# A four-layer network in ten programs in place of seventeen: the start, the joints before self attention, and the experts

## The chip, the cores and the metric

One core of one Trainium2 chip runs the kernel. The metric is the device time of one execution in microseconds (us). The engines are TensorE (PE: matmuls; PEld: its weight loads), VectorE (DVE), ScalarE (ACT), GpSimd (POOL) and SyncE (SP), which here issues all DMAs. Each engine has its own stream of instructions; they meet at semaphores only. A *program* below is one block of five such streams, closed by a barrier over all engines.

## The reference, cut to what matters

The input is x of 8 batches x 256 tokens x 128 features, a condition vector per batch and a context of 8 x 1601 x 128. Layer 0 is, in short:

```python
c_proj = silu(c) @ W_mod + b_mod            # six vectors per batch: shift, scale, gate
x = x + gate_a * (self_attention(modulate(_ln(x), shift_a, scale_a)) @ W_proj + b_proj)
q_c  = _ln(x) @ W_qc + b_qc                 # 16 heads of 8
kv_c = _ln(context) @ W_kvc + b_kvc         # 1601 keys; only this layer normalises the context
x = x + cross_attention(q_c, kv_c) @ W_cproj + b_cproj
x = x + gate_m * (gelu(modulate(_ln(x), shift_m, scale_m) @ W_mlp1 + b_mlp1) @ W_mlp2 + b_mlp2)
```

Layer 1 has rotary positions in the self attention; layer 2 has shifted windows of 64 tokens there (masks), the 16 largest scores alone in the cross attention, and a gated MLP. Layer 3 is

```python
nx = layer_norm(x)
evidence = softmax((nx @ Wq) @ (context @ Wk).T * H**-0.5) @ (context @ Wv)    # one head
combined = concat([nx, evidence, anchor])
router_probs = softmax(combined @ router_W + router_b)                          # three experts
h = silu(combined @ e_w1 + e_b1);  expert_out = h @ e_w2 + e_b2
routed = sum(expert_out * router_probs)
g = sigmoid(silu(combined @ gate_w1 + gate_b1) @ gate_w2 + gate_b2)
out = x + g * (routed @ out_w + out_b)
```

## The kernel before, in words

x stays in SBUF, features on the 128 partitions and 2048 tokens along the columns, worked on in NC = 4 chunks of CH = 512 columns (two batches each). `program` (L2474) runs the stages one after the other, each a program of its own: for each layer `stage_load` (L183: weights, vectors, the modulation vectors), in layer 0 `stage_context_norm` (L248), `stage_project` (L504: the norm of x, the projections to q, k and v, the split of q and k into three bf16 parts), `stage_attention` (L958) for the self attention and again for the cross attention, and `stage_mlp` (L1430: output projection of the cross attention, norm, MLP). Layer 2's cross attention, its MLP and layer 3 up to the evidence are one program, `stage_last` (L1626); then come `stage_load` for layer 3 and `stage_experts` (L2329). q and k go through DRAM (`q_dram`, `k_dram`), and before also v (`v_dram`), since the attention wants them in another layout.

The context norm works batch by batch with two buffers (`cn_raw`, b % 2), 13 tiles of 128 keys. SP loads batch b as soon as the norm and the transposition of b-2 are done, then stores batch b-1 behind its evictions. DVE takes the statistics of b (L292, L296, L299, L301), waits for ScalarE's square root (L324), and normalises b in place:

```python
nc.vector.reciprocal(rv[:, k, :], rv[:, k, :]).then_inc(ve_r.sem, 1)
dve.wait_ge(rstd_r.sem, rstd_r.at(b + 1))
for j in range(NT):
    last = nc.vector.tensor_scalar(raw[:, k, j, :], raw[:, k, j, :], mv[:, k, j, 0:1], rstd[:, k, j:j + 1],
                                   ALU.subtract, ALU.mult)
last.then_inc(norm_r.sem, 1)
```

PE then transposes the 13 tiles (L317), ScalarE evicts them (L331), SP stores them to `ctxn_dram` (L271). The rows of constants that the attention stages need are written by memsets: two on DVE of 10.73 us each (L225) and two on POOL of 13.89 us together (L203) in `stage_load` of layer 0.

In `stage_last` the order of the work is written out by hand: `LastOrder` gives each item of the layer-3 chain of batch b a step (b starts at step 52 b + 72; the evidence loop of scores `x3`, values and denominators is one item per step), and every engine runs through the steps in the same order, its score work first, then the items. Score work of the cross attention ends with step 415 of 416 steps; the chains of batches 6 and 7 run on alone behind it. `stage_experts` takes the four chunks in order; each is 15 uses of a ring of seven PSUM banks: router r0 to r2, then per expert two hidden blocks h (Silu) and an output y, then the gate g1 (Silu), g2 (Sigmoid) and the output o, 28 matmuls of 128x512 in all. The router's exponential (L2419) comes behind r2.

Of the kernel before, what the change touches and what calls it, by code (L numbers as in the profile page):

```python
# [104 lines left out]
class Program:  # L105
    def __init__(self, nc, ctx, io):
# [12 lines left out]
        self.vec = self.sb("vec", [P, V_MAX])  # L119
        self.modv = self.sb("modv", [P, 9, B])  # L120
# [5 lines left out]
        self.v_dram = dram("v_dram", (B, P, 2, NH * VW), F32)  # L126
# [44 lines left out]
def vector(p, layer, name, n=0):  # L171
    at = V_OFF[layer][0][name] + n
    return p.vec[:, at:at + 1]


def stage_load(p, layer):

    nc, (w_off, n_w), (v_off, n_v) = p.nc, W_OFF[layer], V_OFF[layer]
    loaded, act_ready, mm_ready, mod_ready, rows_set = (p.sig(s) for s in ("w_loaded", "cact_ready", "mod_mm", "mod_ready", "rows_set"))
    n_mod = dict(L_WEIGHTS[layer]).get("mod", 0)  # L180
    n_dma = 2 + (5 if layer == 0 else 0)
    scale_slots = [] if layer == 3 else [m[layer][0] for m in (MOD_SELF, MOD_CROSS, MOD_MLP) if m[layer][0] is not None]
    with ExitStack() as ctx:  # L183
        mod_ps = p.ps(f"mod_ps{layer}", [P, 9, B], ctx)
        block = ctx.enter_context(nc.Block())

        @block.sync
        def _(sp):
            sp.dma_start(p.w[:, 0:n_w, :], p.io[f"w{layer}"]).then_inc(loaded.sem, 16)
            sp.dma_start(p.vec[:, 0:n_v], p.io[f"v{layer}"]).then_inc(loaded.sem, 16)  # L190
            if layer == 0:
                sp.dma_start(p.cond[:], p.io["cond"]).then_inc(loaded.sem, 16)
                sp.dma_start(p.const[:], p.io["const"]).then_inc(loaded.sem, 16)
                sp.dma_start(p.neg_id[:], p.io["neg_id"]).then_inc(loaded.sem, 16)
                sp.dma_start(p.id_bf[:], p.io["id_bf"]).then_inc(loaded.sem, 16)
                sp.dma_start(p.x[:], p.io["x"]).then_inc(loaded.sem, 16)
            sp.wait_ge(loaded.sem, loaded.at(16 * n_dma))

        if layer == 0:
            @block.gpsimd  # L200
            def _(pool):
                for hf in range(2):
                    nc.gpsimd.memset(p.q_st[64 * hf + 32:64 * hf + 64], 0.0).then_inc(rows_set.sem, 1)  # L203
                pool.wait_ge(rows_set.sem, rows_set.at(2))
# [2372 lines left out]
```

## Time and profile before

| | |
|---|---|
| time, median of 3 runs | 4627.36 us (4610.62 to 10193.9) |
| the profiled execution | 4624.74 us, span 4623.0 us |
| load and context norm | 0 to 113.3 |
| projection 0, first score of self 0 | 113.3 to 160.1, 166.84 |
| cross 0 ends; MLP 0, load 1, projection 1, first score of self 1 | 956.6; to 1012.4, 1024.3, 1088.7, 1095.5 |
| cross 1 ends; MLP 1, load 2, projection 2, first score of self 2 | 1940.8; to 1998, 2011, 2057.5, 2073.8 |
| the last program: score work, batch 6's and 7's chains | to 4323, 4459.4 |
| load 3 and anchors; four expert chunks | to 4473.6; 4623.0 |
| busy | PE 3625.3, DVE 3536.7, ACT 2945.9, POOL 691.4 us |

Times are positions in the profiled execution, from the start of its span. A profile row gives start and duration of an instruction (a run of equal ones in one row with x and their number), its engine and line, what it writes and reads, and in brackets the idle time of the engine before it and what ended it. SPq is SP's issue of a DMA, not the transfer. A 32-bit matmul shows as two records. The granted clock is a share of TensorE's full 2.4 GHz. The profiled execution is near the median.

### The profile page before, as it was taken

To read this page: it belongs to the slowest core of one execution; us is meant where nothing else is said; L and a number is where in the kernel's file an instruction comes from. 1 tells how busy PE (TensorE), PEld (TensorE's weight loads), DVE (VectorE), ACT (ScalarE), POOL (GpSimd) and SP (SyncE) were. 2 spreads that over 40 slices of the span, in tenths; PEclk is the share of its full clock that TensorE was granted. 3 is DMA by queue.
4 is the path that set the end of the run, shared out by engine and by line. 5 is a ranking of instruction groups with operands and counts; after the bars stand their busy time and mean duration, and the time that the engine had idled before them with its cause. 6 is when DMAs were issued, how large, how long until landed. Compare 5 with 4: busy or idle time off the path is not lost. (4 is left out here: it accounts for less than half of the span.)

```text
span 4623.0 us, 75349 instructions
## 1 busy us (share of the span) xinstructions
PE 3625.3 (78%) x28388; PEld 1609.1 (35%) x28388; DVE 3536.7 (77%) x5424; ACT 2945.9 (64%) x5480; POOL 691.4 (15%) x1464
## 2 busy tenths in 40 slices
PE   2769999976789999858367778787787878778877
PEld 2323333332323333323132334334343434334543
DVE  7658989826568888537699998898989889898213
ACT  1556888844647878627377776767677677766413
POOL 1322122004234242013011010000101000000000
PEclk7788999987879999878666677777777667766769
DMA  4553353205434333144311011110111011000000
GB/s 138 147 132 85 85 112 84 57 22 144 120 91 95 90 94 80 24 107 118 80 36 43 22 29 37 31 34 19 40 30 37 18 32 34 13 12 10 13 19 9
DMA packets 277795, 280.05 MB, mean 61 GB/s; under 512 B 38960, under 2 KB 252472, under 8 KB 276536
## 3 DMA queue, kind: packets, MB, share of 16 engines
q1 hardware_dynamic: 277432, 275.22, 23.9%
q8 instruction: 226, 3.70, 0.4%
q14 instruction: 137, 1.12, 0.1%
HBM read 149.53 MB, written 124.43 MB: 59 GB/s over the span
## 5 line engine op out<-in xcount | busy, mean ns | idle before, releaser
L1369 DVE TENSOR_REDUCE mpart<-ring 128x1 f32<-128x400 f32 (+2 forms) x2816 | 1293.0, 524 | 273.9 <-PE ring L1156 267.1
L1287 ACT ACTIVATE prob<-xa_ps 128x512 f32<-128x512 f32 (+1 forms) x2048 | 1109.8, 596 | 243.5 <-PE xa_ps L1201 223.1
L2068 ACT ACTIVATE prob<-x_ps 128x512 f32<-128x512 f32 (+1 forms) x832 | 451.9, 598 | 313.3 <-PE x_ps L1926 246.5
L1156 PE MATMUL ring<-k_st,q_st 52*128 52x400 bf16 (+2 forms) x2560 | 580.7, 340 | 43.2 <-DMA k_st<-k_dram 11.3
L1790 PE MATMUL ring<-k_st,q_st 52*128 52x400 bf16 (+1 forms) x1024 | 330.5, 444 | 294.2 <-ACT s_sb L2004 276.3
L1220 PE MATMUL xa_ps<-prob,va 128*9 128x256 f32 x6656 | 506.4, 383 | 0.4 <-ACT prob L1287 0.4
L2283 DVE MAX8 mpart<-s_sb 128x8 f32<-128x1601 f32 x256 | 456.1, 1817 | 61.5 <-ACT s_sb L2004 61.5
L2004 ACT ACTIVATE s_sb<-ring 128x400 f32<-128x400 f32 (+1 forms) x1024 | 468.2, 517 | 40.1 <-PE ring L1790 31.8
L1995 ACT ACTIVATE un<-s_sb 128x1601 fp8e4<-128x1601 f32 x256 | 392.9, 1536 | 128.8 <-DVE s_sb L2292 128.3
L2286 DVE MATCH_REPLACE8 s_sb<-mpart,s_sb 128x1601 f32<-128x1601 f32 x256 | 461.9, 1812 | 0.0
L2292 DVE MATCH_REPLACE8 s_sb<-m8b,s_sb 128x1601 f32<-128x1601 f32 x256 | 461.8, 1812 | 0.0
L2289 DVE MAX8 m8b<-s_sb 128x8 f32<-128x1601 f32 x256 | 454.6, 1816 | 0.0
L1201 PE MATMUL xa_ps<-q_st,k_st 55*128 55x256 bf16 (+1 forms) x3840 | 408.6, 279 | 56.7 <-ACT prob L1287 43.5
L1921 PE MATMUL x_ps<-neg_id,un 128*128 128x128 bf16 (+1 forms) x3328 | 349.9, 268 | 47.0 <-ACT prob L2068 46.1
L1921 PEld LDWEIGHTS x_ps<-neg_id,un 128*128 128x128 fp8e4 (+1 forms) x3328 | 286.3, 128 | 188.6 <-ACT prob L2068 131.0
L1943 PE MATMUL av_ps<-prob,va 128*9 128x256 f32 (+1 forms) x3328 | 338.2, 496 | 0.0
L1156 PEld LDWEIGHTS ring<-k_st,q_st 52*128 52x128 bf16 x2560 | 180.1, 95 | 408.5 <-DVE mpart L1369 259.6
L1790 PEld LDWEIGHTS ring<-k_st,q_st 52*128 52x128 bf16 x1024 | 84.8, 112 | 511.8 <-ACT s_sb L2004 387.3
L1201 PEld LDWEIGHTS xa_ps<-q_st,k_st 55*128 55x128 bf16 (+1 forms) x3840 | 142.3, 96 | 314.1 <-ACT prob L1287 287.4
L1926 PE MATMUL x_ps<-q_st,k_st 55*128 55x256 bf16 (+1 forms) x1664 | 210.1, 342 | 0.0
L1271 ACT ACTIVATE mT<-ring 24x128 bf16<-24x128 bf16 x160 | 41.9, 262 | 211.9 <-PE ring L1162 210.3
L1220 PEld LDWEIGHTS xa_ps<-prob,va 128*9 128x9 f32 x6656 | 105.3, 88 | 188.8 <-issue 108.2
(291 smaller groups left out, 4195.3 us busy)
## 6 DMA issues: line engine op xcount, KB each, us to landing
k_st<-kc_dram SPq DMA_DIRECT2D x192, 300.2 KB, 5.5
o_dram<-o_sb SPq DMA_DIRECT2D x192, 128.0 KB, 1.8
kc_dram<-k SPq DMA_DIRECT2D x72, 300.0 KB, 3.4
ctx_t<-in_ctxT SPq DMA_DIRECT2D x24, 800.5 KB, 4.8
q_st<-q_dram SPq DMA_DIRECT2D x80, 192.0 KB, 4.2
kc_dram<-k SPq DMA_DIRECT2D x72, 200.0 KB, 3.9
k_st<-k_dram SPq DMA_DIRECT2D x48, 192.0 KB, 5.0
kc_dram<-k SPq DMA_DIRECT2D x24, 300.8 KB, 3.3
```

Of the source, the lines that this page charges most:

```text
L1156: nc.tensor.matmul(ring_ps[:, r % BANKS, 0:w], q_st[rows, b % NQ, 2 * t + pl, qt * P:(qt + 1) * P], k_st[rows, slot_of(n), pl, c0:c0 + w], ...
L1201: last = nc.tensor.matmul(x_ps[0:sizes[j], (2 * s + hf) % XBANKS, pl * T:(pl + 1) * T], k_st[rows, slot_of(n), pl, keys], q_st[rows, b % N ...
L1220: last = nc.tensor.matmul(av_ps[32 * k:32 * k + VW, n % 2, :], va[0:sizes[j], b % NVB, j, G * t + k, :], prob[0:sizes[j], s % NPROB, (2 * ...
L1287: nc.scalar.activation(prob[0:size, s % NPROB, hf * 512:(hf + 1) * 512], x_ps[0:size, (2 * s + hf) % XBANKS, :], ACT.Exp, scale=HEAD_SCALE ...
L1369: nc.vector.tensor_reduce(mpart[:, n % 4, row, c:c + 1], ring_ps[:, r % BANKS, 0:chunks[c][1]], AX.X, ALU.max).then_inc(g["red"].sem, 1)
L1921: nc.tensor.matmul(x_ps[0:sizes[j], (2 * s + hf) % XBANKS, pq * P:(pq + 1) * P], un[:, n % 2, hf * G + pq, keys], p.neg_id[:], start=pq == ...
L2004: nc.scalar.activation(s_sb[:, q % 4, c0:c0 + w], ring_ps[:, r % BANKS, 0:w], ACT.Copy).then_inc(g["rout"].sem, 1)
L2068: nc.scalar.activation(prob[0:size, s % NPROB, hf * 512:(hf + 1) * 512], x_ps[0:size, (2 * s + hf) % XBANKS, :], ACT.Exp, scale=HEAD_SCALE ...
L2283: ins = nc.vector.max(best, sc)
L2286: ins = nc.vector.match_replace(sc, best, sc, -BIG)
L2289: ins = nc.vector.max(m8b[:, half, :], sc)
L2292: ins = nc.vector.match_replace(sc, m8b[:, half, :], sc, -BIG)
```

## The change

Three parts.

**The start.** `stage_begin` replaces `stage_load` of layer 0 and `stage_context_norm`. SP loads context batches first and puts constants, weights and x between them; POOL does all memsets; the modulation matmuls follow batch 6. The norm goes to ScalarE as Identity with scale = 1/std and bias = -mean/std; DVE computes that bias (`shifts`) in two small operations:

```diff
-                for j in range(NT):
-                    last = nc.vector.tensor_scalar(raw[:, k, j, :], raw[:, k, j, :], mv[:, k, j, 0:1], rstd[:, k, j:j + 1],
-                                                   ALU.subtract, ALU.mult)
-                last.then_inc(norm_r.sem, 1)
+            def shifts(b):
+                k = b % 2
+                dve.wait_ge(rstd_r.sem, rstd_r.at(b + 1))
+                if b >= 2:
+                    dve.wait_ge(norm_r.sem, norm_r.at(b - 1))
+                nc.vector.tensor_scalar(mv[:, k, :, 0], mv[:, k, :, 0], -1.0, None, ALU.mult).then_inc(shift_r.sem, 1)
+                dve.wait_ge(shift_r.sem, shift_r.at(2 * b + 1))
+                nc.vector.tensor_tensor(shift[:, k, :], mv[:, k, :, 0], rstd[:, k, :], ALU.mult).then_inc(shift_r.sem, 1)
+
+            for b in range(B + 1):
+                if b < B:
+                    statistics(b)
+                if b >= 1:
+                    shifts(b - 1)
...
         @block.scalar
+            for b in range(B):
+                k = b % 2
+                act.wait_ge(ve_r.sem, ve_r.at(2 * b + 2))
+                nc.scalar.activation(rstd[:, k, :], rv[:, k, :], ACT.Sqrt).then_inc(rstd_r.sem, 1)
+                if b >= 1:
+                    evict(b - 1)
+                act.wait_ge(shift_r.sem, shift_r.at(2 * b + 2))
+                for j in range(NT):
+                    last = nc.scalar.activation(raw[:, k, j, :], raw[:, k, j, :], ACT.Identity, bias=shift[:, k, j:j + 1], scale=rstd[:, k, j:j + 1])
+                last.then_inc(norm_r.sem, 1)
```

SP's order per batch b is unchanged in kind: load b (behind norm and transposition of b-2), then the store of b-1, which waits for its evictions. DVE's instructions from the start of the context norm, before:

```order
L292 BN_STATS cn_st<-cn_raw 128x6 [waits cn_in1]
L292 BN_STATS cn_st<-cn_raw 128x6 x12
L296 BN_AGGR cn_mv<-cn_st 128x2 [waits cn_stats]
L296 BN_AGGR cn_mv<-cn_st 128x2 x12
L299 TENSOR_SCALAR cn_rv<-cn_mv 128x13 [waits cn_aggr]
L301 RECIPROCAL cn_rv<-cn_rv 128x13 [waits cn_ve]
L304 TENSOR_SCALAR cn_raw<-cn_raw,cn_mv,cn_rs 128x128 [waits cn_rstd]
L304 TENSOR_SCALAR cn_raw<-cn_raw,cn_mv,cn_rs 128x128 x12
```

and of the change, from the statistics of batch 1 on (`cn_in1` is the load of an odd batch, `cn_in0` of an even one):

```order
L248 BN_STATS cn_st<-cn_raw 128x6 [waits cn_in1]
L248 BN_STATS cn_st<-cn_raw 128x6 x12
L252 BN_AGGR cn_mv<-cn_st 128x2 [waits cn_stats]
L252 BN_AGGR cn_mv<-cn_st 128x2 x12
L255 TENSOR_SCALAR cn_rv<-cn_mv 128x13 [waits cn_aggr]
L257 RECIPROCAL cn_rv<-cn_rv 128x13 [waits cn_ve]
L265 TENSOR_SCALAR cn_mv<-cn_mv 128x13 [waits cn_rstd]
L267 TENSOR_TENSOR cn_sh<-cn_mv,cn_rs 128x13 [waits cn_shift]
L248 BN_STATS cn_st<-cn_raw 128x6 [waits cn_in0]
```

The 13 normalising operations are gone from DVE, and the two operations L265 and L267 that stand behind the statistics of batch 1 belong to batch 0.

**Between cross and self stages.** One class `Between` and `stage_between` (L691 of the change) replace `stage_mlp`, `stage_load` and `stage_project`. Its levels run over the four chunks one after the other:

```diff
+    HEAD = ("op", "mean", "var", "diag", "norm", "mod", "up", "down")
+    TAIL = ("mean", "var", "diag", "norm", "proj")
...
+            if self.layer is not None:
+                sp.wait_ge(s["mm"].sem, s["mm"].at(self.at["down", NC - 1] + 1))
+                sp.dma_start(p.w[:, free:n_w, :], p.io[f"w{nxt}"][:, free:n_w, :]).then_inc(s["w2"].sem, 16)
```

All ups come before all downs, through four PSUM banks (before two for the ups and one for the downs, an up and a down of neighbouring chunks in turn). The next layer's weights up to the cross output block are loaded at its start, those that the MLP itself still uses at its end (they serve later stages); vectors and modulation have two places each (`layer % 2`). v stays in SBUF (`vs`), the masks of layer 2 and the first two batches' q and k are loaded in it. On SP, in the joint before self 0, the change has

```order
L156 DMA q_dram<-bt_parts 128x512
L674 DMA q_st<-q_dram 48x8x256 [waits on_st0]
L674 DMA q_st<-q_dram 48x8x256
L683 DMA k_st<-k_dram 48x8x256 x2
L674 DMA q_st<-q_dram 48x8x256 x2
L683 DMA k_st<-k_dram 48x8x256 x2
L156 DMA q_dram<-bt_parts 128x3x512 [waits pj_parts]
```

where before these loads opened the next program. The first line ends the q store of chunk 2, the last begins that of chunk 3; three more stores of k follow.

**The experts beside the last batch.** `LastOrder` gets the expert uses as items of its steps, and `stage_last` the streams of `stage_experts`:

```diff
+        self.experts, self.stores = {}, {}
+        self.weights = self.STEPS * B + 1
+        for c in range(NC):
+            at = self.STEPS * B + 10 + c * N_EXPERT if c < NC - 1 else self.end
+            for n in range(N_EXPERT):
+                self.put(self.experts, at + n, (c, n))
+            self.put(self.stores, at + N_EXPERT + 1, c)
+        self.end += N_EXPERT + 2
```

STEPS x B is 416 and N_EXPERT 15: chunks 0 to 2 take steps 426 to 470, one use a step; batch 6's evidence loop has steps 423 to 437, batch 7's chain 436 to 470 and its loop 474 to 489; chunk 3 comes behind the last evidence. The weights go to the place of the keys (`k_flat`) behind the last score. The expert's intermediate tiles lie in buffers that the scores no longer use, with four PSUM banks (`xa_ps`) in place of seven. The exponential of the router follows h of expert 0 instead of r2. PE in batch 7's chain, before (L1837 and L1844 are its links: root, norm, MLP, mean, variance):

```order
L1837 MATMUL ring<-ls_hid,w 128x256 x4
L1837 MATMUL ring<-x,const 128x256
L1844 MATMUL ring<-const,ls_sqd 128x1 x2
L1837 MATMUL ring<-ls_sqd,const 128x256
```

and in the change (L1838 and L1845 are the same links, L1994 is an expert use, its weights in `k_st` or `s_sb`):

```order
L1838 MATMUL ring<-ls_hid,w 128x256 x4
L1994 MATMUL xa_ps<-nx_190,k_st 128x512
L1994 MATMUL xa_ps<-o_all,k_st 128x512
L1994 MATMUL xa_ps<-prob,k_st 128x512
L1994 MATMUL xa_ps<-s_sb,k_st 128x512
L1838 MATMUL ring<-x,const 128x256
...
L1845 MATMUL ring<-const,ls_sqd 128x1 x2
```

Between two links there are now two to six expert matmuls. On ScalarE, in batch 6's loop, the change reads (L2082 is the loop's exponential, L2159 an expert's Silu or a router logit)

```order
L2082 ACTIVATE ls_hid<-ring 128x256
L2159 ACT_TABLE_LOAD
L2159 ACTIVATE un<-xa_ps,prob 128x256 x2
L2165 ACT_TABLE_LOAD
L2165 ACTIVATE s_sb<-s_sb 128x1536
L2082 ACTIVATE ls_hid<-ring 128x256
L2159 ACT_TABLE_LOAD
L2159 ACTIVATE un<-xa_ps,prob 128x256 x2
L2082 ACT_TABLE_LOAD
L2082 ACTIVATE ls_hid<-ring 128x256 x2
```

where before the loop's exponentials followed one another. From there to the end ScalarE has 26 table loads, before 14.

## Rows read from the trace of the kernel before

**Rows 1.** Page, part 2: the granted clock in 40 slices, tenths of full speed.
```profile
PEclk7788999987879999878666677777777667766769
```

**Rows 2.** Six stretches: start:end length, busy us (x instructions) per engine, clock, DMA share, GB/s.
```profile
28.40:113.30 84.90, 24.23 (x104) 21.09 (x104) 58.98 (x328) 18.67 (x41) 3.51 (x3) 0.70 0.52 155
1012.80:1024.30 11.50, 2.70 (x12) 2.64 (x12) 0.52 (x4) 0.21 (x1) 0.00 (x0) 0.59 0.42 149
4323.00:4333.00 10.00, 7.37 (x41) 2.65 (x39) 4.76 (x9) 1.13 (x3) 0.98 (x5) 0.99 0.09 27
4333.00:4371.00 38.00, 37.94 (x106) 24.50 (x106) 0.35 (x1) 4.61 (x13) 0.72 (x1) 0.50 0.08 26
4414.00:4459.40 45.40, 42.91 (x121) 28.10 (x121) 0.59 (x2) 7.01 (x16) 0.61 (x1) 0.51 0.00 0
4546.00:4581.00 35.00, 26.48 (x57) 11.00 (x58) 13.97 (x15) 14.60 (x27) 0.00 (x0) 0.95 0.02 8
```

**Rows 3.** Timeline of the context norm, batches 1 to 3: start, us, engine, line, operation.
```profile
45.65 0.38 SPq L267 DMA_DIRECT2D cn_raw<-in_ctx  x1
...
52.34 2.61 DVE L292 BATCH_NORM_STATS2 cn_st<-cn_raw 128x6 f32<-128x128 f32 x13 [3.14 <-DMA cn_raw<-in_ctx]
...
56.20 0.24 DVE L301 RECIPROCAL cn_rv<-cn_rv 128x13 f32<-128x13 f32 x1
56.73 3.42 DVE L304 TENSOR_SCALAR cn_raw<-cn_raw,cn_mv,cn_rs 128x128 f32<-128x128 f32 x13 [0.28 <-ACT cn_rs L324]
...
63.85 0.34 SPq L271 DMA_DIRECT2D ctxn_dram<-cn_o  x1
...
64.29 0.38 SPq L267 DMA_DIRECT2D cn_raw<-in_ctx  x1
```

**Rows 4.** Groups of instructions by form, ScalarE, context norm and projection: busy us, mean ns.
```profile
L331 ACT ACTIVATE cn_o<-cn_ps 128x128 f32<-128x128 f32 x8 | 2.2, 272 | 0.0
...
L414 ACT ACTIVATE n_h<-n_xc,modv 128x256 f32<-128x256 f32 x8 | 4.3, 590 | 3.5 <-DVE n_xc L395 3.5
```

**Rows 5.** Timeline at the joints before self 0, self 1 and self 2, single instructions.
```profile
128.72 1.45 PE L556 MATMUL pj_ps<-n_h,w 128*128 128x512 f32 x3
...
156.03 1.57 SPq L164 DMA_DIRECT2D k_dram<-pj_q  x3
...
160.11 0.86 SPq L1036 DMA_DIRECT2D q_st<-q_dram  x2
...
166.84 0.61 PE L1156 MATMUL ring<-k_st,q_st 52*128 52x256 bf16 x4 [5.68 <-DMA k_st<-k_dram]
...
978.12 1.45 PE L1463 MATMUL ml_ps<-n_h,w 128*128 128x512 f32 x3
...
1011.66 0.69 DVE L1496 TENSOR_TENSOR x<-x,ml_res 128x512 f32<-128x512 f32 x1
...
1024.44 1.19 PE L361 MATMUL n_mean<-x,const 128*128 128x512 f32 x1 [0.92 <-PEq L183]
...
1039.93 1.45 PE L556 MATMUL pj_ps<-n_h,w 128*128 128x512 f32 x3
...
1080.43 0.69 DVE L608 TENSOR_TENSOR pj_q<-pj_f,pj_q 128x512 bf16<-128x512 f32 x1
...
1084.56 1.69 SPq L164 DMA_DIRECT2D k_dram<-pj_q  x3
...
2026.48 1.02 PE L556 MATMUL pj_ps<-n_h,w 128*128 128x512 f32 x2
...
2057.59 1.32 SPq L1029 DMA_DIRECT2D q_masked<-in_qmask  x4
...
2073.79 0.61 PE L1156 MATMUL ring<-k_st,q_masked 52*128 52x256 bf16 x4 [15.15 <-DMA k_st<-k_dram]
```

**Rows 6.** Timeline of ScalarE in the tail: a table load and what follows it.
```profile
4386.47 1.28 ACT L2013 ACT_TABLE_LOAD   x1
4387.76 0.47 ACT L2013 ACTIVATE ls_hid<-ring,vec 128x256 f32<-128x256 f32 x1
```

More of the change, by code:

```diff
@@ L539, in _ @@
[L539 to L543 removed]
+            bt.sp(sp)
         @block.tensor
         def _(pe):
[L547 to L556 removed]
@@ L557, in _ @@
-            for g in range(NV):
-                m = NI * stepn + g
-                if g < 3:
-                    pe.wait_ge(pf.sem, pf.at(m - 2))
-                else:
-                    pe.wait_ge(v_out.sem, v_out.at(g - 2))
-                for k in range(4):
-                    last = nc.tensor.matmul(pp[:, m % 3, k * P:(k + 1) * P], norm.h[:, g, k * P:(k + 1) * P], weight(p, layer, "v"), start=True, stop=True)
-                last.then_inc(v_mm.sem, 1)
+            bt.pe(pe)
         @block.scalar
@@ L627, in stage_project @@
-    pf.passed(NI * stepn)
-    for name, mine in turn.items():
-        chain[name].passed(len(mine) * (PER - 1))
-        parts[name].passed(len(mine))
-    stored.passed(16 * len(RUNS) * NI)
-    norm.done()
+            bt.pool(pool)
+    bt.done()
 class Onward:
@@ L900, in by_step, with stage_attention @@
     return out
-def stage_attention(p, layer, kind):
+def stage_attention(p, layer, kind, vs=None, q_self=None):
     nc = p.nc
     cross = kind == "cross"
-    masked = layer == 2 and not cross
     rope = layer == 1
@@ L1519 @@
+N_EXP = 3
+EXPERT_USES = [("r", e, "act") for e in range(N_EXP)]
+for expert in range(N_EXP):
+    EXPERT_USES += [("h", (expert, 0), "act"), ("h", (expert, 1), "act"), ("y", expert, "dve")]
+EXPERT_USES += [("g1", 0, "act"), ("g2", 0, "act"), ("o", 0, "dve")]
+N_EXPERT = len(EXPERT_USES)
 class LastOrder:
@@ L1946, in values, with anchors @@
                 last.then_inc(g["av"].sem, 1)
+            def anchors():
+                pe.wait_ge(g["exp"].sem, g["exp"].at(2 * END))
+                pe.wait_ge(g["ocopy"].sem, g["ocopy"].at(NU))
+                pe.wait_ge(x["w"].sem, x["w"].at(32))
+                pe.wait_ge(x["rw"].sem, x["rw"].at(1))
+                for k in range(10):
+                    if k < 3:
+                        w = e_rw[:, 6 + k, :]
+                    elif k < 9:
+                        w = w_e("ew1", (k - 3) // 2 * 6 + 4 + (k - 3) % 2)
+                    else:
+                        w = w_e("gw1", 2)
+                    last = nc.tensor.matmul(xa_ps[:, 0, k * B:(k + 1) * B], w, p.cond[:], start=True, stop=True)
+                last.then_inc(x["mm"].sem, 1)
@@ L1962, in _ @@
                     values3(b, j)
+                for c, n in order.experts.get(k, []):
+                    if (c, n) == (0, 0):
+                        anchors()
+                    expert(c, n)
         @block.scalar
@@ L2260, in between @@
                     evidence(b)
+                if k == order.weights:
+                    expert_begin()
+                for c, n in order.experts.get(k, []):
+                    if (c, n) == (0, 0):
+                        expert_anchors()
+                    expert_in(c, n)
             def slot(k):
```

1171 lines of the change are left out of this document (561 added, 610 removed).

## The prediction

> **What bounds the kernel now.** I read the page's first two parts, then the chain that ended last, then a table by stretches, and last single instructions in order of time. TensorE's granted clock moves between full and near half over the span [rows 1]. The change leaves the inner loops of the attention stages alone (some 4,000 of the 4,623 us) and rebuilds four places: the start, the three joints before a self attention, and the tail. So I read what ends last in each. In the context norm it is a round trip of load, statistics, norm and transposition, with every engine idle in part: DVE 59 us, PE 24, ACT 19 of 85 us [rows 2]. At the joints a small stage waits for DMAs: the weight load of layer 1 takes 11.5 us for 2.70 us of PE [rows 2]. In the tail first one batch's loop, then the other's, runs on PE at half clock, and the four expert chunks follow alone, the third of them in 35 us [rows 2].
>
> **The start.** Before, a load of batch b is issued (45.65), its statistics start 6.69 us later (52.34), the reciprocal ends at 56.44, the norm on DVE runs from 56.73 to 60.15, and the next store and load are issued at 63.85 and 64.29 [rows 3]. Two batches are in flight, so that this chain of 18.6 us gives two batches, 9.4 us each. What changes is where the norm waits. ScalarE needs the shift of batch b-1, and DVE computes it behind the statistics of b; these wait for load b; SP issues load b+1 only behind the store of b-1, which waits for that norm and its transposition. Nothing of two batches overlaps any more, and each batch pays for the whole chain:
> load to statistics 6.9 (mean of three, 6.69 one of them), statistics to reciprocal 4.10, the two shift operations with their wait 0.5, the norm on ScalarE, and norm end to next load 4.14 [rows 3].
> The norm on ScalarE is 13 operations of 128x128 with scale and bias from columns. No such operation is in the trace. Below it lies the plain copy of 128x128, 0.272; above it the 128x256 with scale and bias, 0.590 alone, which holds twice the columns [rows 4]. In a row of several the latter takes 0.51. I take 0.40, nearer the second because of its two columns; 5.2 us for 13, ends 3.5 and 6.6. It replaces 3.42 on DVE. By the Trainium skill, page "ScalarE: Activation LUTs", a fixed cost and 0.83 ns per column with some 93 ns per pointer operand would make it about 5.0 us, an estimate; this case's rows only enclose it.
> Period: 6.9 + 4.1 + 0.5 + 5.2 + 4.1 = 20.8 us. Load 2 can go out at 24.2 (first statistics at 6.1, second to 14.3, norm 0 to 20.0, 4.1 more). Load 7 goes out five periods later, plus 7 us that the weights (1.4 MB) and x (1 MB) cost on the queue ahead of loads 4 and 6: 135.2. Its statistics, shift, sqrt, the eviction of batch 6, ScalarE's norm with its table switches, and the last store with 3.9 of landing end the program at 168.6. Before, the same point is 113.3 [rows 2], the 28.4 us of the load stage included. **+55.3.** The memsets, now all on POOL, cost nothing: it does nothing else in these 168 us, and together they are some 55 (as long as the two engines took for them before); without that cover a part of these 55 would stand ahead of the first projection.
> Bounds: with the norm at 3.5 or 6.6 the eight periods give -12 or +10.
>
> **The joint before self 0.** The projection starts at 128.72, the last k store is issued at 156.03, the next stage opens at 160.11 and its first score runs at 166.84 [rows 5]: 27.3 + 4.1 + 6.7 = 38.1 us. After, v stays in SBUF, so that no v store stands before the last k store on SP (but eight q and k loads of the first two batches do, 3.7 us, so that I put it at 25.4); those loads land inside the program, and the first score needs only 1.7 after the barrier: 25.4 + 4.2 + 1.7 = 31.3, **-6.8**. The start and this joint together: first score at 215.3 in place of 166.84, +48.5.
>
> **The joint before self 1.** The weights of the next layer load under the MLP. The gap between x ready (1012.35) and the next mean (1024.44) [rows 5] goes: -12.1, of which 2.70 of modulation returns ahead of the up matmuls [rows 2]. All 16 ups before all 16 downs, through four banks in place of two, take 27.3 (32 matmuls of 0.853, if no wait is left) instead of the 34.2 us from 978.12 to 1012.35 [rows 5]: -7.0, and with the modulation the MLP ends 4.4 earlier. The norm that follows need not start at half clock (0.59 in the load stage [rows 2]): I put 13 in place of 15.5, -2.5. From the projection on: from 1039.93 to the k store at 1084.56 44.6, + 4.2 + 6.7 = 55.5 [rows 5]. Now the store goes as soon as DVE has split (1081.12, 41.2), + 4.2 + 1.7 = 47.1: -8.4. Sum -12.1 - 4.4 - 2.5 - 8.4 = **-27.5**.
>
> **The joint before self 2.** The same gap; the MLP with the modulation gains only 1.9, for its first ups are slow for the clock, and that stays. The gap of 13.3 us goes, mean to projection takes 13 in place of 15.4, and x is ready 1.9 earlier: the projection starts at 2008.9 in place of 2026.48, -17.6. Then the masks, four large broadcasts that SP issues first from 2057.59 and that hold the first score till 2073.79 (16.2 us instead of 6.7) [rows 5], move under the MLP: 31.3 in place of 47.3, -16.0. **-33.6.** Cover gone, the masks would cost 9.5.
>
> **The tail.** Before: batch 6's loop ends near 4371, batch 7's chain near 4459.4 [rows 2], load and anchors to 4473.6, four chunks to 4620.5, output to 4623.0. After, chunks 0 to 2 lie between the steps of batches 6 and 7, and the barrier, weight load (9 us) and anchor wait are gone. In three pieces from 4333:
> A, batch 6's loop with anchors and 24 of chunk 0's 28 matmuls. The loop's 37.94 us of PE at clock 0.50 [rows 2] become 19 at full clock, 2.5 more until it rises; anchors 4.4; 24 x 0.853 = 20.5 (a chunk is 28 matmuls, 23.9 of 26.5 busy in its window [rows 2]); waits for softmax and tables some 10. 56 us: 4389.
> B, batch 7's chain to its top scores: 16.7 of PE at full clock, 60 expert matmuls 51.2, waits 13. 81: 4471. The chain's own waits, some 12 us before, lie under expert matmuls.
> C, batch 7's loop, alone and at half clock as before, 47.4 [rows 2]: 4518.5.
> Chunk 3 alone as the last chunk before, 37.8, and the output 2.5: 4558.5.
> Against 4623.0, **-64.5**, ends -35 (30 us of waits more) and -80 (C at a higher clock).
>
> **Sum:** 4623.0 + 48.5 - 27.5 - 33.6 - 64.5 = 4545.9 of span; the profiled execution is 1.74 above its span, so 4547.6, say **4548**, 1.7% under. Against the median 4627.36 the profiled 4624.74 is 0.06% lower, which I neglect.
>
> **Rivals.**
> *ScalarE's table switches hold PE.* In the tail the instruction order has 26 table loads where it had 14, and 16 lie in A and B. A load takes 1.28 us and the next operation starts 0.01 us after it [rows 6], so I count 1.28. If PE waits 2 us more at each of the 16, the tail is 32 longer: 4565 to 4580. For it: in a chunk PE already waits some 7 us for the hidden layer's activations. Against: ScalarE is busy only 14.6 of 35 us [rows 2]. Chance 0.17. The Trainium skill, same page, section "What ACT_TABLE_LOAD costs", adds a drain of about 1,380 ns to the 1,283 of the load; by it the 16 switches make about 22 us, 4570. The rows here show the load's figure and no gap behind it, and the measurement decides.
> *TensorE stays at 1.2 GHz in A and B.* The loop at 4333 ran at 0.50 although the stretch ahead of it was at 0.99, and batch 7's at 0.51, while the third expert chunk got 0.95 [rows 2]. If the mixture is granted what the loop alone was, A becomes 24 longer and B 68: 4640, **slower than before** by 15. It decides once the lower level costs more than 79 us of these 92. Against: more than half of PE's work in A and B is of the kind that ran at 0.95. Chance 0.06 for both, 0.12 for A alone (4572).
> *The start is not serial.* If load b overlaps the norm of b-1, the start costs 15 less than before and not 55 more: about 4480. The order shows the shift behind the statistics, so only 0.04.
> *Fewer waits in the tail, or the clock higher in C:* 4520 to 4535, chance 0.22.
> My forecast with its terms' own scatter, 4535 to 4565, 0.39.
>
> **The numbers.** The likeliest case gives 4548. The range takes in the better tail and the table switches and A alone: 4505 to 4598; outside lie the 1.2 GHz case, the overlapping start and some ends of the terms. Two per cent, about what a measurement of this kernel can tell from no change, is 92.5 us: 4534.8 and 4720. Faster by more: the overlapping start, most of the better tail, and an edge of the forecast, where the start's norm is cheaper: 0.36. Slower by more takes the 1.2 GHz case and a term lost besides: 0.02. The rest, 0.62.
>
> **What would show it.** Right: statistics in the new start begin about 21 us apart, with ScalarE's 13 operations near 5.2; first scores at about 215, and at the joints 27 and 34 us earlier than the shift of the start leaves them; chunk matmuls among batch 7's at a clock near 0.9, and a last chunk of 37 to 38. Wrong: statistics less than 15 apart (the start pipelines), a long idle of PE behind table loads in A and B, or a granted clock near 0.5 from 4333 to the last chunk. A change in the inner loops of the attention stages, of which I expect none, would undo the sum altogether: v now read from one SBUF tensor and ten in place of seventeen programs could move them, and a tenth of a per cent of them is 4 us.

## The result, and the profile after

The changed kernel takes 4593.23 us (median of 19 runs, 4575.58 to 4611.64) against 4630.73 us of the kernel before (19 runs, 4602.85 to 4647.76 but for one of 10193.9, which the ratio leaves out): ratio 0.9925, 95% interval 0.9907 to 0.9942. It is 0.75% faster, clear of noise, where 1.7% was forecast. The profiled execution has a span of 4603.4 us, against the 4545.9 of the sum. It lies in the upper part of its runs, so that the two spans differ by less (19.6 us) than the medians (37.5). The stretches that the change rebuilds repeat better than the total: in the profiles of all kernels below that leave them alone, the first score of self 0 comes at 242.3 to 245.3, the joints take 116.0 to 118.8 and 100.5 to 102.0, the tail 236.1 to 236.2. The attention stretches do not: that of self attention 0 alone lies between 168.6 and 180.2. The comparison goes by stretch:

| stretch | before | predicted | after | after - predicted |
|---|---|---|---|---|
| start to the first score of self 0 | 166.8 | 215.3 | 244.8 | +29.5 |
| self and cross attention 0 | 790.2 | same | 787.8 | -2.3 |
| joint before self 1 (end of cross 0 to first score) | 138.5 | 111.0 | 116.9 | +5.9 |
| self and cross attention 1 | 845.7 | same | 847.2 | +1.6 |
| joint before self 2 | 132.7 | 99.1 | 101.4 | +2.3 |
| layer 2 to batch 6's evidence loop | 2259.3 | same | 2269.2 | +9.9 |
| tail, from that loop on | 289.9 | 225.4 | 236.2 | +10.8 |

The largest miss, half of all, is in the start. DVE's row there, in order of time (the first two batches; columns as in [rows 3], which they answer):

```profile
9.15 0.97 DVE L252 BATCH_NORM_AGGREGATE cn_mv<-cn_st 128x2 f32<-128x6 f32 x13
10.15 8.74 DVE L255 TENSOR_SCALAR cn_rv<-cn_mv 128x13 f32<-128x13 f32 x1
18.93 0.24 DVE L257 RECIPROCAL cn_rv<-cn_rv 128x13 f32<-128x13 f32 x1
19.08 2.55 DVE L248 BATCH_NORM_STATS2 cn_st<-cn_raw 128x6 f32<-128x128 f32 x13
...
22.67 3.20 DVE L255 TENSOR_SCALAR cn_rv<-cn_mv 128x13 f32<-128x13 f32 x1
25.90 0.24 DVE L257 RECIPROCAL cn_rv<-cn_rv 128x13 f32<-128x13 f32 x1
26.06 10.63 DVE L265 TENSOR_SCALAR cn_mv<-cn_mv 128x13 f32<-128x13 f32 x1
36.73 0.17 DVE L267 TENSOR_TENSOR cn_sh<-cn_mv,cn_rs 128x13 f32<-128x13 f32 x1
53.24 2.61 DVE L248 BATCH_NORM_STATS2 cn_st<-cn_raw 128x6 f32<-128x128 f32 x13 [16.34 <-DMA cn_raw<-in_ctx]
```

and POOL's, over the same time:

```profile
1.12 6.92 POOL L235 MEMSET q_st<- 32x8192 bf16 x1
8.10 10.76 POOL L237 MEMSET k_st<- 32x12808 bf16 x1
18.92 6.92 POOL L235 MEMSET q_st<- 32x8192 bf16 x1
25.89 10.77 POOL L237 MEMSET k_st<- 32x12808 bf16 x1
```

Three operations of 128x13 that need 0.1 to 0.2 us last 8.74, 3.20 and 10.63 us, and each ends within 0.04 us of the end of a memset: 10.15 + 8.74 = 18.89 beside 8.10 + 10.76 = 18.86, 22.67 + 3.20 = 25.87 beside 25.84, 26.06 + 10.63 = 36.69 beside 36.66. The statistics between them (19.08, over while a memset runs) are untouched, and so is the reciprocal (18.93, 0.24 us), though it has one tensor input too. What waits is TENSOR_SCALAR, one tensor and a constant. The third batch's statistics start at 53.24; the working has them at 31.1 (load at 24.2, 6.9 more). From there on the start does what was worked out. ScalarE's 13 operations take

```profile
36.94 5.11 ACT L325 ACTIVATE cn_raw<-cn_raw,cn_sh,cn_rs 128x128 f32<-128x128 f32 x13 [17.52 <-DVE cn_sh L267]
```

and the statistics:

```profile
73.97 2.61 DVE L248 BATCH_NORM_STATS2 cn_st<-cn_raw 128x6 f32<-128x128 f32 x13 [16.39 <-DMA cn_raw<-in_ctx]
...
118.79 2.61 DVE L248 BATCH_NORM_STATS2 cn_st<-cn_raw 128x6 f32<-128x128 f32 x13 [16.40 <-DMA cn_raw<-in_ctx]
```

53.24 to 73.97 is 20.7 us (predicted 20.8), 5.11 us for the norm (predicted 5.2, between bounds of 3.5 and 6.6). No weights and no x are loaded ahead of these two batches.

The joints, lines that answer to [rows 5]: the projection of self 0, and the first scores of self 0, 1 and 2.

```profile
206.96 1.88 PE L477 MATMUL bt_bank<-bt_h,w 128*128 128x512 f32 x4
...
244.80 0.61 PE L1214 MATMUL ring<-k_st,q_st 52*128 52x256 bf16 x4
...
1149.52 0.61 PE L1214 MATMUL ring<-k_st,q_st 52*128 52x256 bf16 x4
...
2098.10 0.61 PE L1214 MATMUL ring<-k_st,q_masked 52*128 52x256 bf16 x4
```

From projection to first score 37.8 us where 31.3 was put. From SP's first store to the barrier the DMA view of this stretch (40 slices of 0.74 us, busy tenths and GB/s) reads

```profile
DMA  0699999999999999999999999999999999999940
GB/s 0 208 346 327 350 343 346 322 344 340 335 343 346 328 344 348 315 218 241 177 145 176 176 146 179 155 167 177 146 183 291 386 380 382 382 385 389 382 159 0
```

Between the first and the last slices the DMA engines are never idle: some 340 GB/s in the first stores, about 170 (145 to 241) while the loads pass, and some 380 in seven of the last slices, where the last stores land.

The tail, by stretches (columns as in [rows 2]): batch 6's loop with the anchors and, at its end, the first two expert matmuls; the loop with expert matmuls between its items; batch 7's chain with chunks; its loop alone; chunk 3.

```profile
4367.20:4384.40 17.20, 17.15 (x49) 11.22 (x50) 0.50 (x2) 1.53 (x4) 0.00 (x0) 0.50 0.07 20
4384.40:4418.50 34.10, 32.29 (x118) 18.44 (x117) 9.39 (x8) 22.06 (x33) 0.72 (x1) 0.96 0.05 19
4418.50:4518.40 99.90, 83.58 (x239) 42.17 (x237) 41.69 (x59) 48.04 (x85) 5.78 (x10) 0.95 0.02 8
4518.40:4559.00 40.60, 40.17 (x117) 27.11 (x117) 0.17 (x1) 6.26 (x15) 0.08 (x1) 0.52 0.00 0
4559.00:4603.40 44.40, 31.05 (x58) 12.47 (x58) 14.07 (x15) 16.06 (x27) 0.53 (x1) 0.85 0.02 6
```

Once expert matmuls lie between, the same loop is granted 0.96 where it had 0.50 [rows 2]. The chain with chunks is too long, and its waits are PE's for ScalarE (us in all, times, longest):

```profile
PE xa_ps L1994 <- ACT un L2159: 10.6, 4, 4.3
```

### The profile page after: what moved, and what is told of

The parts are those of the page before. It is cut to its first block, busy times and chain, and to the rows that moved or that the text cites. A ratio compares the mean times of both kernels' runs of the same rounds, so it can differ in the third digit from the quotient of the medians.

```text
span 4603.4 us, 75234 instructions
## 1 busy us (share of the span) xinstructions
PE 3604.8 (78%) x28389; PEld 1598.2 (35%) x28389; DVE 3511.9 (76%) x5334; ACT 2997.1 (65%) x5593; POOL 714.8 (16%) x1466
## 4 chain that ended last, share of the span: by engine, by line
DVE 20%; PE 17%; ACT 10%; issue 3%; POOL 0%; ACTq 0%; POOLq 0%; DVEq 0%
DVE m8b L2448 6%; DVE s_sb L2445 5%; ACT un L2048 5%; DVE s_sb L2451 4%; DVE mpart L2442 3%; PE xa_ps L1922 2%; PE xa_ps L1994 2%; PE ring L1838 2%; ACT prob L2121 2%; PE xa_ps L1944 2%; PE xa_ps L1927 2%; PE ring L1868 2%; ACT s_sb L2057 1%; PE e_ps L1880 1%; PE ring L1791 1%
## 5 line engine op out<-in xcount | busy, mean ns | idle before, releaser
L1343 ACT ACTIVATE prob<-xa_ps 128x512 f32<-128x512 f32 (+1 forms) x2048 | 1109.9, 596 | 245.2 <-PE xa_ps L1259 224.1
L2121 ACT ACTIVATE prob<-xa_ps 128x512 f32<-128x512 f32 (+1 forms) x832 | 452.0, 598 | 313.6 <-PE xa_ps L1927 246.4
L1259 PE MATMUL xa_ps<-q_st,k_st 55*128 55x256 bf16 (+1 forms) x3840 | 408.5, 279 | 54.7 <-ACT prob L1343 43.7
L1922 PE MATMUL xa_ps<-neg_id,un 128*128 128x128 bf16 (+1 forms) x3328 | 351.3, 269 | 46.7 <-ACT prob L2121 45.8
L1922 PEld LDWEIGHTS xa_ps<-neg_id,un 128*128 128x128 fp8e4 (+1 forms) x3328 | 287.1, 128 | 190.8 <-ACT prob L2121 133.4
L1944 PE MATMUL xa_ps<-prob,va 128*9 128x256 f32 (+1 forms) x3328 | 341.4, 501 | 0.0
L1927 PE MATMUL xa_ps<-q_st,k_st 55*128 55x256 bf16 (+1 forms) x1664 | 211.5, 344 | 0.0
```

Of the source, the lines that this page charges most:

```text
L1259: last = nc.tensor.matmul(x_ps[0:sizes[j], (2 * s + hf) % XBANKS, pl * T:(pl + 1) * T], k_st[rows, slot_of(n), pl, keys], q_st[rows, b % N ...
L1343: nc.scalar.activation(prob[0:size, s % NPROB, hf * 512:(hf + 1) * 512], x_ps[0:size, (2 * s + hf) % XBANKS, :], ACT.Exp, scale=HEAD_SCALE ...
L1922: nc.tensor.matmul(x_ps[0:sizes[j], (2 * s + hf) % XBANKS, pq * P:(pq + 1) * P], un[:, n % 2, hf * G + pq, keys], p.neg_id[:], start=pq == ...
L2121: nc.scalar.activation(prob[0:size, s % NPROB, hf * 512:(hf + 1) * 512], x_ps[0:size, (2 * s + hf) % XBANKS, :], ACT.Exp, scale=HEAD_SCALE ...
```

## The experiments

Each starts from the changed kernel. Ratios are to the kernel before, with 95% intervals; "first score" is that of self 0, 244.8 in the changed kernel, "tail" is from batch 6's loop to the end, 236.2. Where the start is left alone its last statistics repeat within 0.3 us. Each position is from one profiled execution.

### 1. Two tensor inputs in place of one

```diff
+ nc.vector.memset(eps[:, 0, :], EPS[0]); nc.vector.memset(eps[:, 1, :], -1.0)
- nc.vector.tensor_scalar(rv[:, k, :], mv[:, k, :, 1], EPS[0], None, ALU.add)
+ nc.vector.tensor_tensor(rv[:, k, :], mv[:, k, :, 1], eps[:, 0, :], ALU.add)
- nc.vector.tensor_scalar(mv[:, k, :, 0], mv[:, k, :, 0], -1.0, None, ALU.mult)
+ nc.vector.tensor_tensor(mv[:, k, :, 0], mv[:, k, :, 0], eps[:, 1, :], ALU.mult)
```

> In the start, the two DVE operations of 128x13 that stood still until a memset of POOL ended (the addition of epsilon, the factor -1) are written with two tensor inputs in place of one tensor and a constant; the memsets stay. Theory (an f32 operation with one tensor input on DVE waits until POOL's running memset is over, one with two inputs does not): these operations take 0.2 us each, the third statistics start near 31 us instead of 53.2 and the first score of self 0 comes near 223 us instead of 244.8, the total 22 us under the changed kernel. Rival (POOL's memsets slow whatever DVE does, by its load on SBUF): the two operations still take 3 to 10 us, the first score stays within 4 us of 244.8.

Measured: first score 222.0, third statistics 31.18, ratio 0.9869 (0.9829 to 0.9909). DVE in order of time, the memsets at the same places as before:

```profile
9.15 0.97 DVE L258 BATCH_NORM_AGGREGATE cn_mv<-cn_st 128x2 f32<-128x6 f32 x13
10.15 0.17 DVE L261 TENSOR_TENSOR cn_rv<-cn_mv,cn_eps 128x13 f32<-128x13 f32 x1
10.36 0.24 DVE L263 RECIPROCAL cn_rv<-cn_rv 128x13 f32<-128x13 f32 x1
10.52 2.55 DVE L254 BATCH_NORM_STATS2 cn_st<-cn_raw 128x6 f32<-128x128 f32 x13
...
14.10 0.17 DVE L261 TENSOR_TENSOR cn_rv<-cn_mv,cn_eps 128x13 f32<-128x13 f32 x1
14.31 0.24 DVE L263 RECIPROCAL cn_rv<-cn_rv 128x13 f32<-128x13 f32 x1
14.46 0.11 DVE L271 TENSOR_TENSOR cn_mv<-cn_mv,cn_eps 128x13 f32<-128x13 f32 x1
...
31.18 2.61 DVE L254 BATCH_NORM_STATS2 cn_st<-cn_raw 128x6 f32<-128x128 f32 x13 [16.39 <-DMA cn_raw<-in_ctx]
```

The same arithmetic takes 0.17 and 0.11 us. The first theory holds to within 1 us: 22.8 us of the miss are these operations. Its wording was too wide, for the reciprocal has one tensor input and takes 0.24 us beside a memset here too (10.36, 14.31): it is TENSOR_SCALAR that waits.

### 2. Memsets half as long

```diff
- nc.gpsimd.memset(p.q_st[64 * hf + 32:64 * hf + 64], 0.0)
+ nc.gpsimd.memset(p.q_st[64 * hf + 32:64 * hf + 64].bitcast(F32), 0.0)
...
- nc.gpsimd.memset(p.k_flat[64 * hf + 32:64 * hf + 64], -1.0)
+ nc.gpsimd.memset(p.k_flat[64 * hf + 32:64 * hf + 64].bitcast(F32), TWO_ONES)    # two bf16 -1 read as one float
```

> The memsets of q_st and k_flat on POOL write the same bytes as 4-byte elements, half as many elements; DVE's operations are untouched. Theory (DVE's one-input operations end when the running memset ends): the memsets fall from 6.9 and 10.8 to about 3.5 and 5.4 us, the blocked operations end with them at about 10, 14 and 20 us, and the first score comes near 229 us instead of 244.8. Rival (the time depends on bytes written, or the blocked time is not tied to the memset's end): first score stays at 245, or moves by another amount than the end of the second k_flat memset moves.

Measured (one run, with no interval): first score 229.9, 0.9 from the number of the theory. The memsets take 3.50 and 5.43 us for the same bytes, and DVE's operations end with them (13.73 + 5.43 = 19.16, and 17.48 + 1.71 = 19.19):

```profile
10.10 3.61 DVE L256 TENSOR_SCALAR cn_rv<-cn_mv 128x13 f32<-128x13 f32 x1
...
17.48 1.71 DVE L256 TENSOR_SCALAR cn_rv<-cn_mv 128x13 f32<-128x13 f32 x1
19.23 0.24 DVE L258 RECIPROCAL cn_rv<-cn_rv 128x13 f32<-128x13 f32 x1
19.38 3.09 DVE L266 TENSOR_SCALAR cn_mv<-cn_mv 128x13 f32<-128x13 f32 x1
```

and POOL:

```profile
4.68 5.43 POOL L238 MEMSET k_st<- 32x6404 f32 x1
10.17 3.51 POOL L236 MEMSET q_st<- 32x4096 f32 x1
13.73 5.43 POOL L238 MEMSET k_st<- 32x6404 f32 x1
```

POOL's memset goes by elements, not by bytes.

### 3. The shifts directly behind their statistics

```diff
-            for b in range(B + 1):
-                if b < B:
-                    statistics(b)
-                if b >= 1:
-                    shifts(b - 1)
+            for b in range(B):
+                statistics(b)
+                shifts(b)
```

> Only DVE's order in the start is changed: the two shift operations of batch b stand directly behind the statistics of b, and no longer behind those of b+1. Theory (serial chain: load b, statistics b, norm b-1, store b-1, load b+1): with this order two batches are in flight again, statistics come 10 to 11 us apart in place of 20.7, the first score falls by 65 to 75 us to about 175 (the memsets still block the first two or three batches for some 20), the whole kernel to about 4525 us, 1.5% under the changed one. Rival (the period of 20.7 is ScalarE's, which has 9.5 us of work a batch, or the DMAs'): statistics stay 18 us apart or more and the first score above 225.

Measured: first score 191.3, ratio 0.9792 (0.9755 to 0.983); statistics of the third to the sixth batch at 46.35, 59.85, 76.76 and 90.29. The serial chain was real (53.5 us for moving two small operations), but the first score lies 16 us above the number expected: the period of batches without other loads fell to 13.5 us and not to 10 or 11, so a part of the theory was missing. ScalarE's order gives a reason: the eviction of b-1 stands behind the square root of b, which waits for the load and the statistics of b. Experiment 5 tests it.

### 4. The norm on DVE

```diff
+                for j in range(NT):
+                    last = nc.vector.tensor_scalar(raw[:, k, j, :], raw[:, k, j, :], mv[:, k, j, 0:1], rstd[:, k, j:j + 1], ALU.subtract, ALU.mult)
...
-                for j in range(NT):
-                    last = nc.scalar.activation(raw[:, k, j, :], raw[:, k, j, :], ACT.Identity, bias=shift[:, k, j:j + 1], scale=rstd[:, k, j:j + 1])
```

> The start stays one program with its order of loads and POOL's memsets, but DVE normalises, as before, directly behind the statistics. Theory: no serial chain, so statistics come 9 to 10 us apart, but the 13 normalising operations have one tensor input and wait for the memsets (38 us of them): the first batch's norm ends near 37 us, and the first score comes at about 160 to 175. Rival (the one-program start itself, not the place of the norm, costs the time): first score above 215.

Measured: first score 197.0, ratio 0.9828 (0.98 to 0.9856). The range for the first score was missed by 22 us: the period is 13.5 here too (41.86, 55.27, 68.80), for the same eviction, and the second statistics come at 41.86, behind all memsets. But the loss against the kernel before (first score 166.8) shrinks from 78 to 30 us, and with ScalarE normalising in the right order (experiment 3) to 24.5: it was the order, not the engine that normalises. The memsets hold DVE here as well: the 13 normalising operations of the first batch take 22.49 us, those of the second 3.42.

### 5. Each batch evicted behind its own norm, with 1 and 3

```diff
                 nc.scalar.activation(rstd[:, k, :], rv[:, k, :], ACT.Sqrt)
-                if b >= 1:
-                    evict(b - 1)
...
+                evict(b)
```

The lines left out are the 13 operations that normalise the batch; those of experiments 1 and 3 are as above.

> The changed kernel's start with three edits: the two-input forms of the first experiment, shifts directly behind the statistics, and ScalarE evicts batch b directly behind its norm, no longer behind the square root of b+1. With the shifts alone moved, statistics came 13.5 us apart and not 10 to 11. Theory: what was left is load b, statistics b, square root b, eviction b-1, store b-1, load b+1 (6.9 + 4.1 + 0.5 + 2 = 13.5); with the eviction moved the period falls to 10 to 10.5 us, the first score to about 157 us, the kernel to some 85 us under the changed one (near 4505 us). Rival (13.5 is the DMAs' own pace for a load and a store of 0.8 MB each, or ScalarE's): the period stays above 12.5, the first score above 172.

Measured: first score 159.0 (157 expected), ratio 0.9735 (0.9713 to 0.9758), 4511.16 us. From the third to the eighth batch the statistics run from 27.64 to 83.06, 11.1 a batch with the weights and x between, where experiment 3 has 46.35 to 119.86, 14.7 a batch. The first of these intervals is 9.4 us (the two rows) for 13.5. By then the memsets are over or, with the two-input forms, hold nothing, so the difference is the eviction's:

```profile
27.64 2.62 DVE L254 BATCH_NORM_STATS2 cn_st<-cn_raw 128x6 f32<-128x128 f32 x13 [6.97 <-DMA cn_raw<-in_ctx]
...
37.01 2.61 DVE L254 BATCH_NORM_STATS2 cn_st<-cn_raw 128x6 f32<-128x128 f32 x13 [4.61 <-DMA cn_raw<-in_ctx]
```

The first score now comes 7.8 us earlier than before, not 78 later, with ScalarE normalising.

### 6. Loads behind the stores, and one batch ahead

```diff
-        for b in range(Q_AHEAD): load_queries(...); load_keys(...)
         for what, c in (("q", 3), ("k", 2), ("k", 3)):
             store(what, c)
+        for b in range(Q_AHEAD): load_queries(...); load_keys(...)
```

> Between cross and self attention, SP issues the q and k loads of the first two batches behind the last three stores in place of ahead of them. Theory (my joints came out 5 us a piece too long because eight loads and the queue's backlog stand ahead of the last stores, which end the program): first scores come 3 to 5 us earlier behind the projection at each joint (after the first projection's start 36.6 now, then 32 to 34). Rival (the landing of whatever comes last sets the end, and the loads take as long to land as the stores): within 1 us of 36.6.

Measured (one run): first score 245.3. From projection to first score the three joints take 38.5, 55.6 and 38.0 us, against 37.8, 52.1 and 37.7 in the changed kernel and 37.2 to 38.3, 52.1 to 53.8 and 35.6 to 37.7 in all that leave them alone. The theory is out: the later loads gain nothing, and the second joint is even 2 us longer. The second kernel takes half of the loads out of the joint:

```diff
-        for b in range(Q_AHEAD):
+        for b in range(1):
             load_queries(p, sp, self.q_self, b, s["loaded"]); load_keys(...)
```

> Between cross and self attention, only batch 0's q and k are loaded inside the joint; batch 1's go at the first step of the self attention. Moving the loads behind the stores had changed nothing (36.6 us from projection to first score at the first joint, with either order), and the DMA engines were busy over 0.9 from the first store to the end. Theory (the joint's end is the work of the DMA engines: 27 us for stores and eight loads, whatever their order): four loads less take 4 to 5 us off each joint, to about 32 us. Rival (a fixed latency of the last store and the barrier): within 1 us of 36.6.

Measured (one run): from projection to first score 33.3 us in place of 37.8 at the first joint, 48.6 in place of 52.1 at the second, 32.5 in place of 37.7 at the third. That is 4 to 5 us at each, outside the scatter just given, so the end of the joint goes by what the DMA engines have to move. (The 36.6 in both expectations counts from a point 1.2 us behind the first projection matmul.) It is no gain: in the self attention PE then waits for the second batch's keys,

```profile
PE ring L1216 <- DMA k_st<-k_dram: 8.4, 1, 8.4
```

which is more than the joint gave. (The first cross attention starts 10.6 us later than in the changed kernel, 427.89 for 417.30; self attention 0 takes 188.6 us, where 168.6 to 180.2 is the scatter of kernels that leave it alone, so not all of the 10.6 is this wait.)

### 7. The tail: exponential later, chunk 2 later, nothing interleaved

```diff
-                    if EXPERT_USES[n][1] == (0, 0):
+                    if EXPERT_USES[n][1] == (0, 1):
                         expert_exp(c)
```

> In the tail alone, ScalarE takes the router's exponential behind both hidden blocks of expert 0 in place of between them. Theory (the two waits of 4.3 us of PE for the hidden block in chunks 1 and 2, and like ones in 0 and 3, are two table loads and the exponential that stand ahead of the second block): each chunk's wait falls from 4.3 to about 1 us, PE does not fall back in clock behind it, the tail gets 12 to 20 us shorter. Rival (ScalarE's work only moves: the same tables are loaded, and the next hidden block waits instead): tail within 5 us of 236.2.

Measured: tail 224.6, 11.6 shorter, just under the range given; ratio 0.9909 (0.9877 to 0.9941). What stood there in the changed kernel, between two hidden blocks of expert 0 (ScalarE):

```profile
4443.69 0.84 ACT L2159 ACTIVATE un<-xa_ps,prob 128x256 f32<-128x256 f32 x2
4444.54 1.28 ACT L2165 ACT_TABLE_LOAD   x1
4445.84 1.48 ACT L2165 ACTIVATE s_sb<-s_sb 128x1536 f32<-128x1536 f32 x1
4447.34 1.28 ACT L2159 ACT_TABLE_LOAD   x1
4448.63 0.84 ACT L2159 ACTIVATE un<-xa_ps,prob 128x256 f32<-128x256 f32 x2
```

Three operations and 4.1 us lie between the two blocks (the first and the last row), each operation starting 0.01 to 0.02 us behind the one ahead. With the exponential later, PE's waits for the hidden blocks in this stretch fall from 10.6 to 3.1 us.

```diff
-            at = self.STEPS * B + 10 + c * N_EXPERT if c < NC - 1 else self.end
+            at = self.STEPS * B + 10 + c * N_EXPERT + 18 * (c == 2) if c < NC - 1 else self.end
```

> In the tail alone, expert chunk 2 moves from steps 456 to 470 (beside batch 7's norms and scores) to steps 474 to 488, beside batch 7's evidence loop, which ran alone in 40.6 us at a granted clock of 0.52; batch 6's loop with expert matmuls between went at 0.96 from its fourth item on. Theory (with expert matmuls between, this loop is granted the full clock too, and takes 20 us of PE and not 40): the stretch with chunk 2 takes about 50 us, the stretch before it loses 20 to 25, the last chunk starts at full clock and saves 3: tail about 222 in place of 236.2. Rival (the waits of the chain, which chunk 2 covered, come back in full, 15 us or more, and eat it): tail 232 to 240.

Measured: tail 224.9, ratio 0.9883 (0.9844 to 0.9921). Batch 7's loop with the whole of chunk 2 between:

```profile
4480.00:4535.00 55.00, 48.98 (x176) 27.32 (x175) 13.98 (x17) 36.21 (x52) 0.98 (x5) 0.97 0.00 0
```

The clock came (0.97 for 0.52), at 55 us. The last chunk was expected to start at full clock and save 3 us; it still began at half clock and took as long as before.

```diff
-            at = self.STEPS * B + 10 + c * N_EXPERT if c < NC - 1 else self.end
+            at = self.end + c * N_EXPERT
-        self.end += N_EXPERT + 2
+        self.end += NC * N_EXPERT + 2
```

> The experts stay in the last program, with their weights loaded early, but all four chunks come behind batch 7's last evidence; nothing of them lies among the chain of batches 6 and 7. Theory (interleaving fills the chain's waits and keeps the granted clock up): chain alone as before 126 us from the first evidence score of batch 6, then four chunks at 35 to 38: the tail is about 275 us, against 236.2 with interleaving and 289.9 before; that puts 14 us on the load and barrier that went and 39 on the interleaving. Rival (the gain is mostly the load and barrier): tail at 245 or less.

Measured: tail 273.5, ratio 1.0004 (0.9995 to 1.0014). Without interleaving the whole change is worth nothing, for the start takes about what the joints and the dropped load (16.4 us of tail) give; the 37.3 us of the interleaving are the gain.

```profile
4353.50:4391.00 37.50, 37.50 (x104) 24.05 (x104) 0.35 (x1) 4.60 (x12) 0.72 (x1) 0.50 0.08 26
4391.00:4434.80 43.80, 31.42 (x113) 20.85 (x112) 10.58 (x25) 13.55 (x26) 4.27 (x10) 0.77 0.00 1
4434.80:4476.00 41.20, 41.19 (x117) 27.39 (x117) 0.00 (x0) 6.23 (x14) 0.00 (x0) 0.50 0.00 1
4476.00:4627.00 151.00, 115.06 (x248) 49.65 (x247) 55.42 (x59) 63.11 (x105) 0.61 (x1) 0.91 0.02 7
```

Both loops are back at 0.50, and the chain between has its waits (31.42 busy of 43.80).

### 8. All that paid

The edits of 1, 3, 5 and the first two of 7 in one kernel.

> The changed kernel with what the runs so far point to: in the start the two-input forms, the shifts directly behind their statistics and each batch evicted behind its own norm; in the tail the router's exponential behind both hidden blocks and chunk 2 beside batch 7's evidence loop. Two batches ahead stay (with one, the self attention waited 8.4 us for batch 1's keys). Theory (the gains are in different places, and add up as far as they do not share a wait): first score at 159, tail at 236.2 - 11.6 - 11.3 = 213 to 217, together 105 us under the changed kernel's profiled span of 4603.4: 4480 to 4505 us as a median, ratio to the kernel before 0.968 to 0.974. Rival (the two tail edits remove the same waits, so that only one counts): tail at 222 or more.

Measured: 4484.4 us (5 runs, 4475.26 to 4496.67), ratio 0.9685 (0.9659 to 0.9711), first score 158.3, tail 212.2. It is 3.15% faster than the kernel before, and the two tail edits add up (236.2 - 11.6 - 11.3 = 213.3).

## Why the prediction was wrong, by its own steps

**The step that failed** is one sentence on the start: "The memsets, now all on POOL, cost nothing: it does nothing else in these 168 us". It looked at POOL, for which there was time, and not at who else is held while POOL works. They cost 22.8 us (experiment 1). ("Some 55" is also no sum of the rows: 38.6 on POOL, and as much on both engines before.) The trace of before could not show it: there the memsets ran beside DVE's own two memsets and ahead of any statistics, and the sum gave no bound for it, only a price for the cover gone. The Trainium skill had the rule, page "SBUF — State Buffer", section "Who interferes with whom": VectorE and GpSimd share a pair of ports; a VectorE operation in a two-port mode, which `tensor_scalar` can enter, and a GpSimd instruction exclude each other for a whole instruction; and an operation with two inputs is free beside a GpSimd instruction that only writes. The runs agree with it: waits to the end of the memset (8.74, 3.20 and 10.63 us), none in the two-input form (0.17 us), none in the statistics and the reciprocal. In which mode an operation ran, no row here shows. That rule spoke against this change and was left out of the prediction.

**The start's chain** was right: 20.8 us a batch, measured 20.7, and moving the shifts alone gives 53.5 us. What a better order would give was understood only with the eviction's place: 14.7 us a batch with the eviction behind the next square root, weights and x included, 11.1 with it behind its own norm.

**The joints**: the direction and the sizes of what went (the weight load, the masks) were right, -21.6 and -31.3 for -27.5 and -33.6. What was mis-sized is the term from the projection to the end of the program. I counted issues on SP and one landing, 25.4 + 4.2 = 29.6 us at the first joint, and it took 37.0; the end goes by the DMA engines' work, which the loads of two batches joined (those of the second batch alone are 4.5 us of it, experiment 6). From projection to first score the three joints are 6.5, 5.0 and 6.4 us longer than put. At the third it is luck that the whole misses by 2.3 only: what lies ahead of the projection came out 4.1 better. Together they miss by 14.7 us: 6.5, 5.9 and 2.3.

**The tail**: A 58 us (56 put), C and chunk 3 89 (88 put), B 89 (81 put). That A and the last piece came out near is luck. In A PE idles for 1.9 us where 10 were put, but the first 17.2 us ran at 0.50, where the rise was to cost 2.5. The loop of C took 44.6 for 47.4 (the window in [rows 2] that it cites is 45.4 long), chunk 3 with the output 44.4 for 40.3: its first 5 us ran at 0.50, so the sign "a last chunk of 37 to 38" failed. In B the waits were as large as put (13), but behind each of the two waits of 4.3 us the next four records of expert matmuls took 3.75 and 3.40 us, where they take 1.88 to 1.96 elsewhere:

```profile
4449.61 3.75 PE L1994 MATMUL xa_ps<-un,k_st 128*128 128x512 f32 x4 [4.29 <-ACT un L2159]
...
4467.76 1.96 PE L1994 MATMUL xa_ps<-un,k_st 128*128 128x512 f32 x4 [1.02 <-ACT un L2159]
```

Of the 8 us of B, these and the slow records behind them are some 4; the rest I could not place. *ScalarE's switches*, the likeliest rival on the slow side, came true in a weaker form: not a price per switch but three operations at one place in each chunk; moving them took 11.6 us away. The Trainium skill, page "ScalarE: Activation LUTs", section "What ACT_TABLE_LOAD costs", adds a drain of about 1,380 ns to each table load. It is not in these rows, where the load starts within 0.02 us of the operation ahead and the next within 0.02 us of the load; the measurement decides. *The 1.2 GHz rival* was wrong: where experts lie between, the grant was 0.96 and 0.95; the loops alone had 0.50 and 0.52. *The start that isn't serial* was wrong for this kernel. One more slip of the working: its bounds for the norm, -12 and +10, are seven periods' and not eight's.

**The stretch that nothing touches**, layer 2 up to the tail, is 9.9 us longer than before. In the other kernels that leave it alone too, it lies anywhere from 2249.3 to 2269.7 us; the kernel before's 2259.3 is inside. It is scatter from one execution to the next, at a granted clock of 0.71 to 0.72; what drives it was not tried.

Of the 57.5 us between the sum and the measured span, 22.8 are thus the memsets, 14.7 the joints, 10.8 the tail and 9.2 the stretches that nothing touches, which are scatter and not a miss of the working.

## What to carry to other kernels

When work goes to an idle engine, ask which instructions of its neighbour stand still meanwhile, by their form, and bound each such wait by the longest instruction that is moved (10.77 us here, and there were three waits). When operations move across a loop's turn, write down the whole round trip (load, both engines, store, next load): two operations of 0.2 us in the wrong place cost 53 us, and an eviction behind the next batch's square root held the batches 14.7 us apart where 11.1 were to be had. At a joint that ends in DMAs, add up the bytes at the rate of the trace, not the issues.

## What the runs showed of the hardware that was not expected

- A TENSOR_SCALAR of DVE (f32, 13 elements a partition) waits for the end of POOL's running memset, up to 10.63 us. The same sum with two tensor inputs takes 0.17 us beside it, and the reciprocal and the statistics, with one tensor input each, are not held either.
- POOL's memset takes as long per element of 4 bytes as of 2: 6.92 and 3.50 us for the same bytes.
- The evidence loop keeps PE busy 99% of the time and is granted 0.50 to 0.52; with expert matmuls between its items it is granted 0.96 and 0.97.
- In the joint before self 0, stores of q and k move at 340 to 380 GB/s, and while their loads pass the rate is about 170 GB/s.
